# Edge attention kernel: maxima subtracted and slots halved by adding DMAs, tile buffer by halves and sides, five deep

## The reference

```python
w_m = (efeat @ W_msg + b_msg).reshape(E, in_f, -1)
w_a = (efeat @ W_attn + b_attn).reshape(E, in_f, -1)
h_src = feat[src][:, :, None]
e1 = w_m * h_src
e2 = w_a * h_src
seg_max = jax.ops.segment_max(e2, dst, num_segments=N)
ex = jnp.exp(e2 - seg_max[dst])
denom = jax.ops.segment_sum(ex, dst, num_segments=N)
attn = ex / denom[dst]
ft = jax.ops.segment_sum(e1 * attn, dst, num_segments=N)
x = layernorm(x + ft.sum(axis=1))
```

## Time and profile before

| | |
|---|---|
| median of 3 runs | 1732.97 us |
| profiled execution, its own time | 1732.84 us |
| its span | 1731.0 us |
| busy: PE, DVE, ACT, POOL | 78%, 89%, 51%, 56% |
| tiles | 110 |

### The profile page before, as it was taken

The page is one execution under the profiler, slowest core; times in us unless marked ns, Lnnn a source line. Parts: engine busy times, 40 slices in busy tenths (PEclk is TensorE's granted clock), DMA queues, the critical chain, the costliest instruction groups (busy, mean ns, idle before and its releaser), DMA issues. The chain is left out here.

```text
span 1731.0 us, 20720 instructions
## 1 busy us (share of the span) xinstructions
PE 1354.0 (78%) x5767; PEld 690.3 (40%) x5767; DVE 1537.4 (89%) x1614; ACT 889.1 (51%) x1842; POOL 974.1 (56%) x878
## 2 busy tenths in 40 slices
PE   0002899999999999999999999999999999998400
PEld 0001444444444444444444444444444444444200
DVE  8534899999999999999999999999999999998458
ACT  1002566666666666666666666666665555554100
POOL 5777777777676676776777676676661000000170
PEclk9999899999999999999999999999999999999655
DMA  4314344444444444444444444444443222221150
GB/s 109 76 19 112 93 122 117 125 122 117 126 119 116 127 119 117 127 118 116 128 118 117 127 118 117 127 118 118 126 116 105 94 81 80 95 71 54 56 147 18
DMA packets 174990, 182.94 MB, mean 106 GB/s; under 512 B 47056, under 2 KB 130328, under 8 KB 174878
## 3 DMA queue, kind: packets, MB, share of 16 engines
q1 hardware_dynamic: 140958, 158.74, 29.1%
q0 software_dynamic: 33920, 22.89, 8.3%
HBM read 92.36 MB, written 89.41 MB: 105 GB/s over the span
## 5 line engine op out<-in xcount | busy, mean ns | idle before, releaser
L488 POOL DMA_INDIRECT split<-x_parts,edge_src x784 | 880.6, 1123 | 351.3 <-issue 220.1
L781 PE MATMUL bank_sum<-em,row_onehot 128*128 128x512 f32 x1760 | 891.4, 609 | 31.3 <-ACT sum_rows L647 31.0
L1024 DVE TENSOR_TENSOR em<-bank_prod,h_rows 128x1024 f32<-128x1024 f32 x440 | 524.2, 1212 | 64.1 <-PE bank_prod L769 58.1
L781 PEld LDWEIGHTS bank_sum<-em,row_onehot 128*128 128x128 f32 x1760 | 299.0, 189 | 222.8 <-issue 184.1
L1042 DVE TENSOR_TENSOR em<-em 128x1024 f32<-128x1024 f32 x220 | 267.7, 1217 | 3.5 <-ACT em L606 3.5
L769 PE MATMUL bank_prod<-w_rows,partsT 100*128 100x512 bf16 x880 | 269.3, 388 | 1.0 <-DMA partsT<-tile_table 0.6
L647 ACT COPY sum_rows<-bank_sum 128x512 f32<-128x512 f32 x220 | 126.8, 576 | 275.6 <-PE bank_sum L781 254.6
L1067 DVE TENSOR_TENSOR em<-em,bank_max 128x2048 f32<-128x2048 f32 x110 | 250.7, 2279 | 3.2 <-ACT node_max L638 3.2
L606 ACT ACTIVATE em<-em 128x2048 f32<-128x2048 f32 x110 | 210.5, 1914 | 3.6 <-DVE em L1067 3.6
L630 ACT COPY chunk_fwd<-bank_max 128x512 f32<-128x512 f32 x110 | 64.5, 586 | 276.7 <-PE bank_max L712 276.7
L769 PEld LDWEIGHTS bank_prod<-w_rows,partsT 100*128 100x128 bf16 x880 | 86.7, 99 | 249.2 <-issue 203.1
(11 more groups left out here) (165 smaller groups left out, 1171.0 us busy)
## 6 DMA issues: line engine op xcount, KB each, us to landing
sums<-sum_rows SPq DMA_DIRECT2D x110, 512.0 KB
rec<-split_records SPq DMA_DIRECT2D x220, 144.0 KB, 2.2
split_records<-split SPq DMA_DIRECT2D x97, 288.0 KB, 2.1
mask<-tile_table SPq DMA_DIRECT2D x110, 192.0 KB, 3.2
split<-x_parts,edge_src POOLq DMA_INDIRECT x784
rel<-tile_table SPq DMA_DIRECT2D x110, 64.0 KB, 3.0
edge_feat<-in_features SPq DMA_DIRECT2D x97, 64.0 KB
flag<-tile_table SPq DMA_DIRECT2D x110, 2.0 KB
```

Of the source, the lines that this page charges most:

```text
L488: return nc.gpsimd.indirect_dma_start(out, None, src, bass.IndirectOffsetOnAxis(idx, 0))
L781: mm = nc.tensor.matmul(bank_sum[:, :], row_onehot[:, t % RING, g, :], em[:, t % RING, s * GROUPS + g, :, :, :].rearrange("p i m o -> p (i ...
L1024: V.tensor_tensor(em[:, v, 2 * j:2 * j + 2, :, :, :].rearrange("p s i m o -> p s i (m o)"), bank_prod[j % 2][:, :, :].rearrange("p s (i x) ...
```

## The change

`em` gets a ring of 5 and the layout `em[P, ring, half, side, 4 (slot, group), 256]`: half 0 has slots 0 and 1, half 1 slots 2 and 3; side 0 is attention, side 1 message. The weight matrices are laid out to match. `shift` is removed from DVE. ACT writes the negated maxima twice over into `minus_max` (`negate_maxima`), and POOL issues a DMA that adds them to the attention side of both halves (`subtract_maxima`). After `weigh`, POOL issues a DMA that adds half 1 to half 0 (`add_halves`), and PE sums 2 slots in place of 4. POOL's gathers are set between these two in its own tile loop. `h_rows` is written twice over for the two sides; some small tables now lie in the last part of `em`; `rec_max` is negated once on DVE before it is turned, as it now holds negated maxima.

```diff
+EM_RING = 5
+HALF = SIDE // 2
-        em = sb("em", [P, RING, SIDE, FEAT, 2, FEAT])
+        em = sb("em", [P, EM_RING, 2, 2, HALF, ATT])
-        node_max = sb("node_max", [P, 2, GROUPS * ATT])
+        minus_max = sb("minus_max", [P, 2, HALF * ATT])
...
# POOL
-            for q in range(PREP_FIRST, PREPS):
-                gather_features(q)
+            def gather_some(q, edges):
+                if not prep(q):
+                    return
+                u, n = q % PREP_RING, prep_rows(q)
+                if edges[0] == 0:
+                    pool.wait_ge(in_landed[u], 32 * (q // PREP_RING + 1))
+                for e in edges:
+                    at = H_AT + H_WORDS * (e % SLOTS)
+                    gather(split[0:n, u, e // SLOTS, at:at + H_WORDS], xs_d,
+                           edge_src[0:n, u, e:e + 1]).then_inc(h_landed[u], 16)
+            def subtract_maxima(t):
+                pool.wait_ge(neg_ready, t + 1)
+                nc.gpsimd.dma_start(em[:, t % EM_RING, :, 0, :, :].rearrange("p h k x -> p h (k x)"),
+                                    bc(minus_max[:, t % 2, :], 1, [P, 2, HALF * ATT]),
+                                    accum_op=ALU.add).then_inc(shift_landed[t % 2], 16)
+            def add_halves(t):
+                pool.wait_ge(weighted, 2 * (t + 1))
+                e = em[:, t % EM_RING, :, :, :, :].rearrange("p h m k x -> p h (m k x)")
+                nc.gpsimd.dma_start(e[:, 0, :], e[:, 1, :], accum_op=ALU.add).then_inc(added[t % 2], 16)
+            for t in range(FIRST, LAST + 1):
+                gather_some(t + LEAD, range(0, 5))
+                subtract_maxima(t)
+                gather_some(t + LEAD, range(5, 7))
+                add_halves(t - 1)
+                gather_some(t + LEAD, range(7, 8))
...
# ACT
-                act.wait_ge(shifted, t + 1)
+                act.wait_ge(shift_landed[t % 2], rounds(t, 2))
...
-                nc.scalar.copy(node_max[:, t % 2, :], bank_max[:, :]).then_inc(max_copied, 1)
+                    act.wait_ge(shift_landed[t % 2], rounds(t - 2, 2))
+                nc.scalar.activation(minus_max[:, t % 2, :].rearrange("p (s y) -> p s y", s=2),
+                                     bc(bank_max[:, :], 1, [P, 2, GROUPS * ATT]), ACT.Copy, scale=-1.0).then_inc(neg_ready, 1)
...
-                exponents(t - 1)
                 copy_parts(t + 2)
+                exponents(t - 1)
...
# PE
-                since(pe, shifted, t)
+                since(pe, neg_ready, t)
...
+                if pair == 0:
+                    pe.wait_ge(added[t % 2], rounds(t, 2))
+                    pe.wait_ge(onehot_ready, 2 * (t + 1))
+                    since(pe, sums_copied, 2 * t + g)
+                mm = nc.tensor.matmul(bank_sum[:, :].rearrange("p (m x) -> p m x", m=2), row_onehot[:, t % RING, g, :],
+                                      em[:, t % EM_RING, 0, :, pair * GROUPS + g, :], start=(pair == 0), stop=(pair == 1))
...
                 turn_maxima(t)
                 give_parts(t + 2)
-                sum_slots(t - 2, 0, [0])
                 products(t + 1, 2)
                 give_features(t + 2)
-                sum_slots(t - 2, 0, [1])
+                sum_slots(t - 2, 0, 0)
                 products(t + 1, 3)
-                sum_slots(t - 2, 0, [2])
+                sum_slots(t - 2, 0, 1)
                 turn_back(t)
-                sum_slots(t - 2, 0, [3])
                 products(t + 2, 0)
+                sum_slots(t - 2, 1, 0)
                 pick_ends(t)
-                sum_slots(t - 2, 1, [0])
                 products(t + 2, 1)
-                sum_slots(t - 2, 1, [1, 2, 3])
+                sum_slots(t - 2, 1, 1)
...
# DVE
-                    since(v_eng, sums_ready, 2 * (t - RING + 1))
+                    since(v_eng, sums_ready, 2 * (t - EM_RING + 1))
...
-                V.tensor_tensor(e, e, bc(m, 1, [P, SLOTS, GROUPS * FEAT, FEAT]), ALU.subtract).then_inc(shifted, 1)
...
-                shift(t)
```

More of the change, by code:

```diff
@@ L213, in region @@
             return em_flat[:, at:at + k * width].rearrange("p (k r) -> p k r", k=k)
+        spare = em[0:TILES, EM_RING - 1, :, :, :, :].rearrange("p h m k x -> p (h m k x)")
+        table = spare[:, 0:COLUMNS * WIDE].rearrange("p (j c) -> p j c", c=COLUMNS)
+        filled = spare[:, COLUMNS * WIDE:2 * COLUMNS * WIDE].rearrange("p (c j) -> p c j", c=COLUMNS)
+        c_a, c_b, c_first, c_end = [spare[:, (2 * COLUMNS + k) * WIDE:(2 * COLUMNS + k + 1) * WIDE] for k in range(4)]
         r_rows = region(0, 4, BOTH)
@@ L223, in gnn_kernel @@
         fin = region(0, NODE_COLS, BOTH)
+        f_sum, f_mid = [region(NODE_COLS * BOTH + a * NODE_COLS * FEAT, NODE_COLS, FEAT) for a in range(2)]
+        out_rows = em_flat[:, NODE_COLS * (BOTH + 2 * FEAT):NODE_COLS * (BOTH + 3 * FEAT)]
         iotas = sem("iotas")
@@ L283, in gnn_kernel @@
         max_back = sem("max_back")
-        max_copied = sem("max_copied")
+        neg_ready = sem("neg_ready")
         recmax_stored = [sem(f"recmax_stored{u}") for u in range(2)]
-        shifted = sem("shifted")
+        shift_landed = [sem(f"shift_landed{u}") for u in range(2)]
+        added = [sem(f"added{u}") for u in range(2)]
         exp_done = sem("exp_done")
@@ L295, in gnn_kernel @@
         recmax_landed = sem("recmax_landed")
+        recmax_turned = sem("recmax_turned")
         recmax_ps = sem("recmax_ps")
@@ L514, in _ @@
                 gather_features(q)
-            for q in range(PREP_FIRST, PREPS):
-                gather_features(q)
+            def gather_some(q, edges):
[9 more added lines that the diff above has]
+            def subtract_maxima(t):
+                if not tile(t):
+                    return
+                pool.wait_ge(neg_ready, t + 1)
[3 more added lines that the diff above has]
+            def add_halves(t):
+                if not tile(t):
+                    return
+                pool.wait_ge(weighted, 2 * (t + 1))
[7 more added lines that the diff above has]
+                gather_some(t + LEAD, range(7, 8))
             for u in range(OUT_RING):
@@ L621, in copy_features @@
                 since(act, times_h, 4 * (t - 1))
-                nc.scalar.copy(h_rows[:, t % 2, :, :].rearrange("p g k -> p (g k)"),
-                               bank_t[0][:, 0:GROUPS * SLOTS * FEAT]).then_inc(h_copied, 1)
+                rows = bank_t[0][:, 0:GROUPS * SLOTS * FEAT].rearrange("p (y k) -> p y k", k=FEAT)
+                nc.scalar.copy(h_rows[:, t % 2, :, :, :, :].rearrange("p g s m k -> p (g s) m k"),
+                               bc(rows, 2, [P, GROUPS * SLOTS, 2, FEAT])).then_inc(h_copied, 1)
             def copy_forward(t):
@@ L630, in copy_forward, with negate_maxima @@
                 nc.scalar.copy(chunk_fwd[:, :], bank_max[:, :]).then_inc(fwd_copied, 1)
-            def copy_maxima(t):
+            def negate_maxima(t):
                 if not tile(t):
@@ L650, in _ @@
                 q = t + LEAD
+                copy_parts(t + 2)
                 exponents(t - 1)
-                copy_parts(t + 2)
                 part1(q)
@@ L657, in _ @@
                 copy_sums(t - 2, 0)
-                copy_maxima(t)
+                negate_maxima(t)
                 end_places(t + 1)
@@ L771, in products, with sum_slots @@
                 mm.then_inc(prod_ready, 1)
-            def sum_slots(t, g, slots):
+            def sum_slots(t, g, pair):
                 if not tile(t):
                     return
-                if slots[0] == 0:
-                    pe.wait_ge(weighted, 2 * (t + 1))
+                if pair == 0:
+                    pe.wait_ge(added[t % 2], rounds(t, 2))
                     pe.wait_ge(onehot_ready, 2 * (t + 1))
                     since(pe, sums_copied, 2 * t + g)
[L780 to L784, removed]
+                mm = nc.tensor.matmul(bank_sum[:, :].rearrange("p (m x) -> p m x", m=2), row_onehot[:, t % RING, g, :],
+                                      em[:, t % EM_RING, 0, :, pair * GROUPS + g, :], start=(pair == 0), stop=(pair == 1))
+                if pair == 1:
                     mm.then_inc(sums_ready, 1)
@@ L1020, in times_features @@
                     v_eng.wait_ge(h_copied, t + 1)
-                    since(v_eng, sums_ready, 2 * (t - RING + 1))
+                    since(v_eng, sums_ready, 2 * (t - EM_RING + 1))
                 v_eng.wait_ge(prod_ready, 4 * t + j + 1)
[L1023 to L1026, removed]
+                k = 2 * (j % 2)
+                h = h_rows[:, t % 2, :, j, :, :]
+                V.tensor_tensor(em[:, t % EM_RING, j // 2, :, k:k + 2, :].rearrange("p m k (i o) -> p k m i o", o=FEAT),
+                                bank_prod[j % 2][:, :, :].rearrange("p k (m i o) -> p k m i o", m=2, o=FEAT),
+                                bc(h, 4, [P, GROUPS, 2, FEAT, FEAT]),
+                                ALU.mult).then_inc(times_h, 1)
             def run_forward(t):
@@ L1040, in weigh @@
                 v_eng.wait_ge(exp_done, t + 1)
```

(9 more changed lines are left out.)

47 lines of the change are left out of this document (16 added, 31 removed).

## The result

The changed kernel takes 3340.05 us (median of 4 runs, 3336.15 to 3350.72) against 1732.95 us: a ratio of 1.929, 95% interval 1.924 to 1.934. It is slower by the closed chain that was forecast, but by 580 us more than the forecast of 2760 us, and 50 us beyond the upper end of the range, 3290 us.

What follows compares the result with a forecast made beforehand. DVE's load was taken to bound the kernel before. After: 88 rounds of 22.8 us and 22 of 20.2, plus 303.2 outside, 3 drain, 1 negation and 1.8 offset, gave 2760 us; range 2150 to 3290.

Steps and rivals of the forecast that it cites:

- closed chain: PE, ACT and POOL: twelve pieces each waiting for the one before, from sums to add's landing; round 22.8 us.
- The first reading: DVE: shift and a 0.44 us pause go, leaving 10.34 us a tile, 1440 us if the replacement is hidden.
- 1 to 4, with the clock: PE's first two sum_slots, products and turn_back up to copy_forward's start: 2.9 us, plus 2.8 at the lower clock.
- 5, ACT's three: ACT in order: copy_forward, row_places and copy_sums, 2.23 us.
- 6 and 7: PE: wake-up and sum_slots(.,1,0), then pick_ends to ACT's start; full clock assumed, though the lower could cost 1.9 us.
- 9, 10: subtract's issue, gathers: POOL: issuing the subtract, 1.3 us, then two gathers before the add, 2.6 us.
- D: POOL's time to issue one new transfer: taken 1.3 us, bounds 0.9 and 2.3.
- A: Piece 12, landing of the add's data after issue: taken 6.5 us, between 4.3 and 11.
- the upper end, 11 us: Add's landing: 5.4 us data, 1.6 fixed, 2 for the subtract still draining, 2 for mixed traffic.
- Rival (b): Slow adds: half rate and queueing behind the subtract, A 10.5, rounds 26.8 and 24.2, 3199 us; chance 20%.
- The clock: PE: drops to 1.2 GHz after waiting 9.5 us for the add, adding 2.8 us to pieces 1 to 4.
- The subtract's loop: Negation, subtract, exponent, next copy_forward: about 10.3 us from negation to there, where the chain gives 14.7.

Runs made afterwards that it cites:

- e3: Changed kernel with POOL issuing the add of tile t-1 ahead of the subtract of tile t: 2743.5 us.
- e4: Changed kernel with PE's sums, ACT's copies out and SP's stores one round later (t-3 in place of t-2): 2566.8 us.
- experiment two: Changed kernel, POOL's order: two gathers moved from between subtract and add to behind the add, 3312.6 us; or add ahead of subtract (e3), 2743.5 us.
- e7b_warm: Changed kernel plus 13 constant matmuls a round on PE, 7 ahead of give_features and 6 behind it: 3096.3 us.
- e10_flags_first: Changed kernel without the adding of halves (PE sums four slots), with SP's flag loads ahead of its preparation store: 1954.5 us, against 2229.3 without that move.
- five: Experiment on small loads: chain of waits in the changed kernel with the subtract DMA alone, 2229.3 us; flag loads moved ahead (e10_flags_first), 1954.5 us.

## Why the prediction was right or wrong

*The first reading, 1440 us.* DVE lost 232 us of the 250 forecast. PE does 880 instructions fewer, as worked out, but its busy time did not fall (1354.0 and 1361.3 us): at a mean granted clock of 0.69 in place of 0.96 the rest takes longer. Neither was on the path, and the saving counted for nothing, as foreseen.

*The closed chain.* Right: the profile shows the twelve pieces in order, and two different cuts (e3, e4) take 597 and 773 us off.

*The terms of the round.* Against the measured round:

| pieces | predicted us | measured us |
|---|---|---|
| 1 to 4, with the clock | 2.9 + 2.8 = 5.7 | 4.66 (1448.95 to 1453.61) |
| 5, ACT's three | 2.23 | 2.24 |
| 6 and 7, taken at full clock | 2.15 | 3.81 |
| 8, negation | 1.03 | 1.03 |
| 9, 10: subtract's issue, gathers | 1.3 + 2.6 | 4.21 with wake-up |
| 11, 12: add's issue D + A | 1.3 + 6.5 = 7.8 | 11.93 |
| round | 22.8 | 27.88 |

*D and A, the step that failed.* The mechanism was right, and the term A, piece 12, was too small: taken at 6.5 us, "nearer the plain copy", it is 11.93 - 1.02 = 10.9 us. D was about right, 1.3 and 1.0 us. I had both parts of the truth in the upper end, 11 us: half the rate, and the subtract still draining. The larger miss is the second. Without the subtract ahead of it the add needs 7.3 us with its issue, 6.3 behind it, so 6.5 was the size of an add that waits for nobody; the wait for the subtract's data, which the forecast left out and the upper end put at 2 us, is 4.6. Rival (b) was doubted because DMA engines were idle more than half of the time; but how idle an engine is says nothing of how long one transfer through it takes. The one measured twin, 390 GB/s, was of a copy. Rival (b) with A = 10.5 is what happened, at 3199 us.

*What was left between 3199 and 3340.* The subtracts' issues start at 196.04 us, the 89th at 2626.80 and the last at 3200.32. So the first 88 rounds take 27.62 us each where rival (b) has 26.8, together some 72 us, and the last ones 27.31 where it has 24.2, some 68 us. In the round of the table, pieces 6 and 7 at the lower clock are 1.7 us more than forecast, left out on purpose and wrongly (in some rounds they ran at full speed, 1.10 and 0.88 us at 1483.58), and pieces 1 to 4 are 1.0 us less. In the tiles without gathers I took off 2.6 us each; they lost much less, since the add then waits longer behind the subtract (experiment two). The upper end had a slip too: its own terms, rounds of 27.7 and 25.1 us, add up to 3299 us and not to 3290, and the measured time lies beyond both. With pieces 6 and 7 at the lower clock the range would have held it.

*The clock.* It fell as forecast: pieces 1 and 2 ran at 1.2 GHz in this round (2.08 and 0.85 us), 3 and 4 partly or no longer, 6 and 7 again, which was not forecast. In all it is at least 2.2 us a round by `e7b_warm` against 2.8 forecast.

*The subtract's loop.* Forecast as shorter than the chain; right, 15.1 us in `e10_flags_first`. But the loop that came next was not it: the small flag loads, late beside the adding transfer (five). Nothing of it was in the prediction.

*The order of ACT.* `copy_parts` ahead of `exponents` was in the diff, and I gave it no term. It is the only part of this change that gains: 23 us (1730.95 to 1707.86).

## What to carry to other kernels

Before work goes from a busy engine to a DMA, close the loop: write down who waits for the landing and what it issues next, and add up one round with the landing in it. Price an adding DMA at half of a copy's rate, some 5.5 us of data per MiB here in place of 2.6, plus whatever drains ahead of it: here that wait, 4.6 us, was the larger part of what the forecast lacked. Small loads that went out behind a store and beside it got late as well, so issue them first, and let whoever needs a landing wait for it a full round later.

## What was not expected of the hardware

- A 1 MiB adding DMA within SBUF moved at 189 GB/s, a copying one of the same shape at 398 GB/s; alone in its kernel the add moved at 198 GB/s (33.3% of 2184.2 us less 143.7, for 115.3 MB).
- A 1 MiB add landed 7.3 us after its issue alone, 11.9 us when it was issued 3.9 us behind another, and 14.5 us when 0.8 us behind it.
- A 2 KB load took 6.9 us to land while an adding transfer and a 288 KB store drained, where a 144 KB one took 2.2 us before.
- POOL's issue of the subtract took 1.31 us adding and 0.74 us copying.
- 13 idle-time matmuls of a constant per tile made a kernel 7% faster (3340 to 3096 us); the mean granted clock rose from 0.69 to 0.94.
